# A routing chain interleaved with side work, one choice's columns built by ScalarE, activation tables loaded early and weight loads held for the first gathered rows

## The chip, the cores and the metric

The kernel runs on one core of a Trainium2 chip. The core has five engines: TensorE (PE in the profile) multiplies matrices out of SBUF into PSUM, its weight loads are listed as PEld; VectorE (DVE), ScalarE (ACT) and GpSimd (POOL) work element by element; SyncE (SP) issues transfers. Each engine runs its own instruction list in order, and they meet at semaphores. Transfers run on 16 DMA engines. TensorE's clock is granted at one of two levels, 1.2 and 2.4 GHz; the profile shows it as 0.5 and 1.0. The metric is the device time of one execution in microseconds (us).

## What is computed

A gated cross-attention block and a gated mixture of experts, both with a residual. Cut to what matters:

```
x = x + tanh(g_xattn) * xattn(layernorm(x), ctx)          # x: 16 x 112 x 256, ctx: 16 x 375 x 192, 16 heads
xf = layernorm(x) as 1792 rows of 256
probs = softmax(xf @ router_w.T)                            # 8 experts
topv, topi = top_k(probs, 2); probs = probs * mask; probs = probs / (probs.sum + 1e-9)
h = silu(xf @ gate_w[e] + gate_b[e]) * (xf @ up_w[e] + up_b[e])     # 256 -> 512
y = sum over e of probs[e] * (h @ down_w[e] + down_b[e])            # 512 -> 256
x = x + tanh(g_ffn) * y
```

## The kernel before

`attention` (to 315 us) computes the first line, batch by batch, in 20 software-pipelined steps, and leaves x, its row means and variances (mv2) and the raw router logits (routed) in SBUF. In its last steps ScalarE has only copies and squares to do.

`experts` follows. Its first part is the **routing**, written as one chain on VectorE in a layout of 112 partitions x 16 batches x 8 experts: inverse deviation (ScalarE does the Sqrt, L1245), logits, maximum, Exp on ScalarE (L1247), then twice "maximum, equal, tie-break, maximum, select" (L1420 to L1429) for the two choices of each row, and `both`, the mask of the two. From `both` TensorE counts the rows of each expert and ranks them; VectorE turns this into pos, the place of each row and choice in a list sorted by expert (L1442 to L1456). The list has 21 tiles of 256 places. To turn it round (which row stands at place p?) pos is split into chunk and offset, and TensorE multiplies two one-hot matrices: `col` (line == offset, 128 columns) and `chunks` (line == chunk, times value), for choice 1 first and then for choice 0 (L1325 to L1332). The result plus a constant is `slot_row` (L1480), the row numbers that the gather needs. Every operation of the chain is issued through `link`, which gives the operation a semaphore and waits for it at once, also where the next operation doesn't need its result.

Beside the chain ScalarE normalises x in place (XW, L1252, 16 activations), SyncE writes it to `xn_scr` in DRAM in four stores (L1180), and GpSimd, after the stores and slot_row, gathers rows with indirect transfers (L1046, two for each tile, four tiles ahead). SyncE's list ahead of the stores: weights of the first one and a half experts (w_raw x3, DL x2), small biases, zero rows, dbB; behind them DL of the third expert, and then the loop of weight loads (L1182), each waiting until VectorE has used up the buffer it goes to (e_l).

Then come the **tiles**, software-pipelined: in step c, TensorE transposes tile c (L1343), does gate and up of tile c-1 (L1366) and down of tile c-2 (L1381). ScalarE makes xH, the high part of the rows (L1263), sg = Silu(gate) (L1278), hH (L1290) and the weighted ys (L1301); VectorE makes xL (L1506), hf = (up + bias) * sg (L1527), hL (L1538) and ys (L1549). The weights, too, are split on chip while the first 8 tiles run: `high` (L1021, GH) on ScalarE and `low` (L1033, GL) on VectorE, numbered 2e for the gate and 2e+1 for the up weights of expert e, and `down_high` (L1026, DH) and `down_low` (L1040, DL). TensorE's gate and up of tile t wait for low(2t+1) (`e_l`, L1357). For expert 1, low(2) is in step 0 and low(3) in step 1 on VectorE, behind the first hf and xL.

## Time and profile before

| | |
|---|---|
| median of 3 runs (range) | 563.6 us (563.16 to 569.83) |
| profiled execution: time, span | 564.71 us, 562.9 us |
| mean granted clock of TensorE | 0.933 |
| busy: PE, PEld, DVE, ACT, POOL | 471.5, 430.2, 409.8, 317.0, 298.1 us |

The page cuts the span into 40 slices of 14.1 us; a digit is the busy share of a slice in tenths. Slices 23 to 25 (from 310 us) are the stretch of the routing:

```profile
PE   2986899999999999999988324799899999999920
DVE  4875989999999989999995585687865545555510
ACT  4651556667577566757555732777855455455410
PEclk9998999999999999999997655899999999999975
DMA  9566687775676576474311685567624433433333
```

In rows of a timeline: start in us, busy us, engine, line, operation, output<-inputs, shapes, count, and in brackets the idle time of the engine before it with what ended it.

### The profile page before, as it was taken

The page shows a single profiled execution, that of the slowest core. Times are in us where ns is not written, and L with a number is a line of the kernel's source. Part 1 is how long each engine was busy: PE and PEld are TensorE (multiplying, and loading weights), DVE is VectorE, ACT ScalarE, POOL GpSimd, SP SyncE. Part 2 cuts the span into 40 slices and gives each one's busy share as a digit, 9 for nine tenths or more (in the row PEclk, how much of TensorE's full clock was granted, in tenths as well). Part 3 has the DMA queues.
Part 4 walks back from the last instruction along what each step waited for, and adds up shares of the span by engine and source line. Part 5 has one row for each costly group of instructions (what it writes and reads, how often), then busy time and mean ns, then how long its engine had stood idle before and what let it go on. Part 6 is the DMA issues. An engine that isn't in the chain of part 4 may idle for free. (4 is left out here: it accounts for less than half of the span.)

```text
span 562.9 us, 15096 instructions
## 1 busy us (share of the span) xinstructions
PE 471.5 (84%) x4723; PEld 430.2 (76%) x4724; DVE 409.8 (73%) x872; ACT 317.0 (56%) x606; POOL 298.1 (53%) x268
## 2 busy tenths in 40 slices
PE   2986899999999999999988324799899999999920
PEld 2865898999889999999867313698799999999820
DVE  4875989999999989999995585687865545555510
ACT  4651556667577566757555732777855455455410
POOL 5093456666556666755675208034657765654440
PEclk9998999999999999999997655899999999999975
DMA  9566687775676576474311685567624433433333
GB/s 203 158 170 147 148 193 176 182 184 123 173 174 148 118 173 182 109 178 109 85 53 57 203 273 191 176 199 204 141 51 75 76 47 66 65 55 48 39 38 130
DMA packets 69022, 74.88 MB, mean 133 GB/s; under 512 B 28744, under 2 KB 57248, under 8 KB 68784
## 3 DMA queue, kind: packets, MB, share of 16 engines
q1 hardware_dynamic: 60912, 63.23, 43.1%
q0 software_dynamic: 8064, 11.06, 12.0%
q8 instruction: 27, 0.44, 0.3%
q14 instruction: 19, 0.16, 0.1%
HBM read 42.51 MB, written 14.98 MB: 102 GB/s over the span
## 5 line engine op out<-in xcount | busy, mean ns | idle before, releaser
L365 POOL TENSOR_TENSOR PL<-PT 125x448 f16<-125x448 f32 x112 | 109.5, 985 | 102.9 <-ACT PT L495 102.8
L495 ACT ACTIVATE PT<-bank 125x448 f32<-125x448 f32 x192 | 100.8, 543 | 86.2 <-PE bank L626 85.9
L783 DVE TENSOR_REDUCE mx<-bank 112x1 f32<-112x375 f32 x256 | 124.8, 538 | 18.6 <-PE bank L608 17.8
L1236 POOL DMA_INDIRECT acc_scr<-ys,slot_row x42 | 66.9, 1594 | 83.8 <-ACT ys L1301 73.7
L626 PE MATMUL bank<-QS,KS 98*125 98x256 f32 x384 | 82.8, 305 | 4.8 <-DMA QS<-nm 3.7
L608 PE MATMUL bank<-KS,QS 97*112 97x376 f32 x256 | 79.9, 352 | 2.9 <-DVE mx L783 2.2
L1527 DVE SCALAR_TENSOR_TENSOR hf<-bank,ub,sg 128x256 f32<-128x256 f32 x84 | 38.4, 482 | 51.9 <-ACT sg L1278 51.8
L1366 PE MATMUL bank<-xH,GH 128*128 128x256 f16 x336 | 66.1, 279 | 7.7 <-DVE GL L1033 3.6
L626 PEld LDWEIGHTS bank<-QS,KS 98*125 98x125 f32 x384 | 63.7, 193 | 6.5 <-DMA QS<-nm 4.0
L1366 PE MATMUL bank<-xL,GH 128*128 128x256 f16 x336 | 65.7, 278 | 0.0
L1366 PE MATMUL bank<-xH,GL 128*128 128x256 f16 x336 | 65.4, 277 | 0.0
L1046 POOL DMA_INDIRECT xt<-xn_scr,slot_row x42 | 45.4, 1082 | 30.8 <-DVE slot_row L1480 18.3
L773 DVE TENSOR_TENSOR PL<-PT 125x448 f16<-125x448 f32 x80 | 56.6, 707 | 5.6 <-ACT PT L495 5.3
L645 PE MATMUL bank<-VS,PT 125*128 125x49 bf16 x768 | 52.2, 189 | 4.0 <-POOL PL L365 1.9
L1278 ACT ACTIVATE sg<-bank,gb,inv 128x256 f32<-128x256 f32 x84 | 42.7, 560 | 20.1 <-PE bank L1366 20.0
L645 PE MATMUL bank<-VS,PL 125*128 125x49 bf16 x768 | 50.4, 186 | 0.0
L608 PEld LDWEIGHTS bank<-KS,QS 97*112 97x112 f32 x256 | 44.6, 177 | 7.2 <-DVE mx L783 5.3
L645 PEld LDWEIGHTS bank<-VS,PT 125*128 125x128 bf16 x768 | 38.2, 99 | 15.4 <-issue 3.1
L1301 ACT ACTIVATE ys<-ys,slot_weight 128x256 f32<-128x256 f32 x42 | 19.1, 500 | 42.9 <-DVE ys L1549 41.0
L1366 PEld LDWEIGHTS bank<-xH,GH 128*128 x336 | 32.3, 99 | 13.9 <-issue 9.4
L1538 DVE TENSOR_TENSOR hL<-hf,hH 128x1024 fp32r<-128x1024 f32 x21 | 25.9, 1233 | 16.9 <-ACT hH L1290 11.3
L645 PEld LDWEIGHTS bank<-VS,PL 125*128 125x128 f16 x768 | 38.1, 97 | 0.0
(214 smaller groups left out, 1033.9 us busy)
## 6 DMA issues: line engine op xcount, KB each, us to landing
KS<-kH SPq DMA_DIRECT2D x128, 94.0 KB, 2.7
KS<-kL SPq DMA_DIRECT2D x64, 94.0 KB, 2.2
QS<-q_scr SPq DMA_DIRECT2D x96, 56.0 KB
ctx_sb<-in_ctx SPq DMA_DIRECT2D x16, 281.2 KB
wsq<-in_L_ffn_gate_w SPq DMA_DIRECT2D x8, 512.0 KB, 3.9
wsq<-in_L_ffn_up_w SPq DMA_DIRECT2D x8, 512.0 KB, 5.0
w_raw<-in_L_ffn_gate_w SPq DMA_DIRECT2D x8, 512.0 KB, 4.2
w_raw<-in_L_ffn_up_w SPq DMA_DIRECT2D x8, 512.0 KB, 3.9
```

The source lines that it names most:

```text
L365: pool.tensor_tensor(PL[:, 2 * k:2 * k + 2, :, 0:N], PT[:, 2 * k:2 * k + 2, :, 0:N], PH[:, 2 * k:2 * k + 2, :, 0:N], ALU.subtract).then_in ...
L495: act.activation(PT[:, 2 * k:2 * k + 2, :, 0:N].rearrange("p a e i -> p (a e) i"), psST[k % 2][0:JP].rearrange("p (a i) -> p a i", i=NI)[: ...
L608: pe.matmul(psS[hd % SBANKS][0:N, 0:MP], QS[u][0:RM, hd // 2, hd % 2, 0:N], KS[u][0:RM, hd // 2, :], start=True, stop=True).then_inc(p_S, 1)
L626: mm = pe.matmul(psST[k % 2][0:JP, 2 * NI * a:2 * NI * (a + 1)], KS[u][0:RM + 1, p, JP * t:JP * (t + 1)], QS[u][0:RM + 1, p, :, :].rearran ...
L645: mm = pe.matmul(psO[0][:, VW * (hd % 8):VW * (hd % 8 + 1)], P[:, JT * p + t, e, :], VT[:, u, t, hd, :], start=(part == 0 and t == 0), sto ...
L773: dve.tensor_tensor(PL[:, 2 * k:2 * k + 2, :, 0:N].rearrange("p a e i -> p (a e) i"), PT[:, 2 * k:2 * k + 2, :, 0:N].rearrange("p a e i -> ...
L783: dve.tensor_reduce(mx[:, hd:hd + 1], psS[hd % SBANKS][0:N, 0:M], AX.X, ALU.max).then_inc(v_max, 1)
L1046: pool.indirect_dma_start(xt[:, t % XR, k, :], None, xn_scr, bass.IndirectOffsetOnAxis(ap=slot[:, TH * t + k:TH * t + k + 1].bitcast(U32), ...
L1236: pool.indirect_dma_start(acc_scr, bass.IndirectOffsetOnAxis(ap=slot[:, TH * t + k:TH * t + k + 1].bitcast(U32), axis=0), ys[:, u, k, :], ...
L1278: act.activation(sg[:, f, :], bG[f // FB][:, TS * (f % FB):TS * (f % FB + 1)], ACT.Silu, bias=gb[:, bass.ds(e * FC + f, 1)], scale=inv[:, ...
L1366: mm = pe.matmul(bank[:, TS * (f % FB):TS * (f % FB + 1)], w.rearrange("p o f -> p (o f)"), x[:, u, k, :], start=(n == 0 and k == 0), stop ...
L1527: dve.scalar_tensor_tensor(out=hf[:, f, :], in0=bU[f // FB][:, TS * (f % FB):TS * (f % FB + 1)], scalar=ub[:, bass.ds(e1 * FC + f, 1)], in ...
```

## The change

- **Chain.** `link` is split in `mark` (gives the semaphore) and the wait. The sum of the exponentials, m12, den and rden move from behind `both` in between the links of the two choices. Behind pos the small operations are issued in an order in which neighbours don't depend on each other, and each waits only for what it reads.
- **Columns.** `col` of choice 0 is made by ScalarE: 16 activations |offset - line| of 112x128 and one Relu(1 - that) over all 2048 elements. `offset` becomes F32. TensorE waits for ScalarE there.
- **Tables.** Two activations with an unread result: a Sqrt of two elements in step 17 of attention, and a Silu behind the first down_high.
- **Weights.** SyncE waits for the first tile's gathered rows (l_x[0]) before its loop of weight loads; low(3) moves on VectorE from step 1 to step 0.

```
+                    if isinstance(i, int) and NB * i + c == B + 1:
+                        act.activation(v["unread"][:], ident[:, 0:2], ACT.Sqrt)
...
-            chunk, offset = tmp("k_chunk", [N, 2, B], BF16), tmp("k_offset", [N, 2, B], BF16)
+            chunk, offset = tmp("k_chunk", [N, 2, B], BF16), tmp("k_offset", [N, 2, B], F32)
...
                 load_down(sp, 2)
+                sp.wait_ge(l_x[0], 16 * TH)
                 for n in range(WB, 2 * E):
...
+                act.wait_ge(e_off, 1)
+                act.wait_ge(q_k, 9)
+                for b in range(B):
+                    ins = act.activation(col[:, 0, b, :], line[:], ACT.Abs, bias=offset[:, 0, b:b + 1], scale=-1.0)
+                ins.then_inc(a_col, 1)
+                act.wait_ge(a_col, 1)
+                act.activation(col[:, 0].rearrange("i b l -> i (b l)"), col[:, 0].rearrange("i b l -> i (b l)"),
+                               ACT.Relu, bias=ones[0:N, 0:1], scale=-1.0).then_inc(a_col, 1)
                 act.wait_ge(e_sc, 1)
                 high(act, 0)
                 high(act, 1)
                 down_high(act, 0)
+                act.activation(v["unread"][:], ident[:, 0:2], ACT.Silu)
...
-                    pe.wait_ge(e_col, n + 1)
+                    if k == 1:
+                        pe.wait_ge(e_col, 1)
+                    else:
+                        pe.wait_ge(a_col, 2)
...
-                link(dve.tensor_reduce(r["sum"][:], R["exp"][:], AX.X, ALU.add))
-                link(dve.tensor_tensor(r["m12"][:], r["m1"][:], r["m2"][:], ALU.add))
-                link(dve.scalar_tensor_tensor(out=r["den"][:], in0=r["sum"][:], scalar=1e-9, in1=r["m12"][:],
-                                              op0=ALU.mult, op1=ALU.add))
-                link(dve.reciprocal(r["rden"][:], r["den"][:]))
+                dve.wait_ge(e_r, n_rden)
...
+                n_mid = mark(dve.tensor_scalar(k2["mid"][:], k2["pos"][:], -63.5, 1.0 / 128, ALU.add, ALU.mult))
+                n_near = mark(dve.tensor_scalar(k2["near"][:], k2["pos"][:], 0.5 - TS / 2, 1.0 / TS, ALU.add, ALU.mult))
+                dve.wait_ge(e_r, n_mid)
+                n_chunk = mark(dve.tensor_scalar(chunk[:], k2["mid"][:], EDGE, EDGE, ALU.add, ALU.subtract))
...
-                                if arrived(i, c):
+                                if arrived(i, c) and UN * i + c > 1:
                                     low(dve, 2 * (UN * i + c) + 1)
...
                     if arriving(i, c):
                         low(dve, 2 * (UN * i + c + 1))
+                        if not has(i, c, 1):
+                            low(dve, 2 * (UN * i + c + 1) + 1)
```

ScalarE's list from the first activation of the expert phase to the first tile, before; XW is the normalised x, GH and DH are high parts of weights, xH the rows of tile 0, k_offset is offset:

```order
L1245 ACT_TABLE_LOAD
L1245 ACTIVATE rstd<-veps 112x16 [waits dve_ve2]
L1247 ACT_TABLE_LOAD
L1247 ACTIVATE r_exp<-r_low 112x128 [waits dve_low]
L1252 ACTIVATE XW<-XW,shift,rstd 112x256 [waits attention_stored0,dve_shift]
L1252 ACTIVATE XW<-XW,shift,rstd 112x256 x12
L1252 ACTIVATE XW<-XW,shift,rstd 112x256 [waits attention_stored1]
L1252 ACTIVATE XW<-XW,shift,rstd 112x256 x2
L1021 ACTIVATE GH<-w_raw,sc 128x1024 [waits gate_in0,dve_scale]
L1021 ACTIVATE GH<-w_raw,sc 128x1024 [waits gate_in1]
L1026 ACTIVATE DH<-DL 128x1024 [waits down_in0]
L1263 ACTIVATE xH<-bank 128x512 [waits pe_tileT]
```

The same place in the changed kernel:

```order
L1251 ACTIVATE rstd<-veps 112x16 [waits dve_ve2]
L1253 ACT_TABLE_LOAD
L1253 ACTIVATE r_exp<-r_low 112x128 [waits dve_low]
...
L1258 ACTIVATE XW<-XW,shift,rstd 112x256 x2
L1263 ACTIVATE col<-line,k_offset 112x128 [waits pool_constants,dve_offset]
L1263 ACTIVATE col<-line,k_offset 112x128 x15
L1266 ACTIVATE col<-col,ones 112x2048 [waits act_col]
L1025 ACTIVATE GH<-w_raw,sc 128x1024 [waits gate_in0,dve_scale]
L1025 ACTIVATE GH<-w_raw,sc 128x1024 [waits gate_in1]
L1030 ACTIVATE DH<-DL 128x1024 [waits down_in0]
L1272 ACT_TABLE_LOAD
L1272 ACTIVATE unread<-ident 128x2
```

One table load is gone at the head, 17 activations stand between XW and the first weights, and a table load stands ahead of xH.

VectorE's list over steps 0 and 1 of the tiles, before; the step border is the TENSOR_LOAD of the tile's expert, hf is the product with sg:

```order
L1511 TENSOR_TENSOR both_w<-xt,slot_choice 128x4 [waits tile_in0]
L1514 TENSOR_REDUCE slot_weight<-both_w 128x2 [waits dve_two_weights]
L1040 TENSOR_TENSOR DL<-DL,DH 128x1024 [waits act_down_high]
L1033 SCALAR_TENSOR_TENSOR GL<-w_raw,sc,GH 128x1024 [waits act_high]
L1151 TENSOR_LOAD tile_e
...
L1506 SCALAR_TENSOR_TENSOR xL<-bank,xH 128x512 [waits act_tile_x]
L1511 TENSOR_TENSOR both_w<-xt,slot_choice 128x4 [waits tile_in1]
L1514 TENSOR_REDUCE slot_weight<-both_w 128x2 [waits dve_two_weights]
L1033 SCALAR_TENSOR_TENSOR GL<-w_raw,sc,GH 128x1024 [waits act_high]
L1527 ISA [waits act_silu]
L1527 SCALAR_TENSOR_TENSOR hf<-bank,ub,sg 128x256
```

The same place in the changed kernel:

```order
L1553 TENSOR_TENSOR both_w<-xt,slot_choice 128x4 [waits tile_in0]
L1556 TENSOR_REDUCE slot_weight<-both_w 128x2 [waits dve_two_weights]
L1044 TENSOR_TENSOR DL<-DL,DH 128x1024 [waits act_down_high]
L1037 SCALAR_TENSOR_TENSOR GL<-w_raw,sc,GH 128x1024 [waits act_high] x2
L1156 TENSOR_LOAD tile_e
...
L1548 SCALAR_TENSOR_TENSOR xL<-bank,xH 128x512 [waits act_tile_x]
L1553 TENSOR_TENSOR both_w<-xt,slot_choice 128x4 [waits tile_in1]
L1556 TENSOR_REDUCE slot_weight<-both_w 128x2 [waits dve_two_weights]
L1569 ISA [waits act_silu]
L1569 SCALAR_TENSOR_TENSOR hf<-bank,ub,sg 128x256
```

The GL behind tile 1's xL now stands in step 0, behind the other one.

SyncE's list behind the stores, before and then changed, where the first load of the loop gets one more wait (tile_in0 is l_x[0]):

```order
L1180 DMA xn_scr<-XW 112x4x258 [waits act_xn2] x3
L1015 DMA DL<-in_L_ffn_down_w 128x4x256
L1012 DMA w_raw<-in_L_ffn_up_w 128x2x512 [waits dve_wlow]
L1015 DMA DL<-in_L_ffn_down_w 128x4x256
L1012 DMA w_raw<-in_L_ffn_gate_w 128x2x512 [waits dve_wlow]
```

```order
L1185 DMA xn_scr<-XW 112x4x258 [waits act_xn2] x3
L1019 DMA DL<-in_L_ffn_down_w 128x4x256
L1016 DMA w_raw<-in_L_ffn_up_w 128x2x512 [waits dve_wlow,tile_in0]
L1019 DMA DL<-in_L_ffn_down_w 128x4x256
L1016 DMA w_raw<-in_L_ffn_gate_w 128x2x512 [waits dve_wlow]
```

Nothing changed its place there; every later load stands behind the new wait.

## Rows read from the trace of the kernel before

**Rows 1.** Windows: busy us (instructions) of each engine, then PEclk, DMA share, GB/s.

```profile
333.00:335.00 2.00, 0.09 (x2) 0.00 (x0) 2.00 (x2) 0.00 (x0) 0.00 (x0) 0.50 1.04 323
```

**Rows 2.** Timeline of ScalarE, end of attention and routing.

```profile
307.96 0.42 ACT L449 ACTIVATE xc<-XW 112x256 f32<-112x256 f32 x1 [1.02 <-DVE XW L845]
...
315.08 1.28 ACT L1245 ACT_TABLE_LOAD   x1 [0.98 <-PEq L246]
...
317.92 0.31 ACT L1247 ACTIVATE r_exp<-r_low 112x128 f32<-112x128 f32 x1
318.13 7.95 ACT L1252 ACTIVATE XW<-XW,shift,rstd 112x256 f32<-112x256 f32 x16
325.99 2.17 ACT L1021 ACTIVATE GH<-w_raw,sc 128x1024 f16<-128x1024 f32 x2
```

**Rows 3.** Timeline of VectorE, routing chain.

```profile
322.17 0.28 DVE L1432 TENSOR_REDUCE s_sum<-r_exp 112x16 f32<-112x128 f32 x1
...
323.19 0.40 DVE L1438 SCALAR_TENSOR_TENSOR XW<-s_m,tg,s_rden 112x16 f32<-112x16 f32 x2
...
326.17 0.18 DVE L1458 TENSOR_SCALAR k_mid<-k_pos 112x32 f32<-112x32 f32 x1
...
327.71 0.86 DVE L1469 TENSOR_TENSOR chunks<-line,k_chunk 112x672 f16<-112x672 bf16 x1
...
333.25 2.29 DVE L1475 TENSOR_TENSOR col<-line,k_offset 112x2048 bf16<-112x2048 bf16 x1
...
336.44 0.20 DVE L1480 TENSOR_TENSOR slot_row<-bank,spare 128x42 int32<-128x42 f32 x1 [0.90 <-PE bank L1329]
```

**Rows 4.** Source line L1180 in 325.9 to 327, the last store.

```profile
L1180 SPq DMA_DIRECT2D xn_scr<-XW x1: 305/305/305, 326.1 to 326.1; - x1
...
DMA to landing us min/median/max: 8.8/8.8/8.8
```

**Rows 5.** Timeline round the gather; last, DMA busy tenths from 337, slices of 0.2 us.

```profile
337.57 1.17 POOL L1046 DMA_INDIRECT xt<-xn_scr,slot_row  x1 [18.28 <-DVE slot_row L1480]
...
338.15 2.47 DVE L1033 SCALAR_TENSOR_TENSOR GL<-w_raw,sc,GH 128x1024 f16<-128x1024 f32 x2
339.04 1.22 POOL L1046 DMA_INDIRECT xt<-xn_scr,slot_row  x1 [0.30 <-issue]
339.45 0.39 SPq L1012 DMA_DIRECT2D w_raw<-in_L_ffn_up_w  x1
...
340.54 1.22 DVE L1040 TENSOR_TENSOR DL<-DL,DH 128x1024 fp32r<-128x1024 f32 x1
340.57 2.01 POOL L1046 DMA_INDIRECT xt<-xn_scr,slot_row  x1 [0.30 <-issue]
...
343.90 1.11 PE L1343 MATMUL bank<-ident,xt 128*128 128x128 f32 x4 [7.51 <-DMA xt<-xn_scr,slot_row]
...
DMA  0000000000009351072149899998999999987899
```

**Rows 6.** The chain (first row, start and us), ScalarE and TensorE at tiles 0, 1.

```profile
346.52 6.32 PE bank L1366 x24
...
352.96 1.28 ACT L1278 ACT_TABLE_LOAD   x1 [4.29 <-PE bank L1366]
...
358.17 0.61 PE L1366 MATMUL bank<-xH,GH 128*128 128x256 f16 x2 [3.56 <-DVE GL L1033]
```

**Rows 7.** Timeline of VectorE, hf of tiles 0, 1, 2 and 3.

```profile
354.97 0.94 DVE L1527 SCALAR_TENSOR_TENSOR hf<-bank,ub,sg 128x256 f32<-128x256 f32 x2 [4.89 <-ACT sg L1278]
...
363.46 0.88 DVE L1527 SCALAR_TENSOR_TENSOR hf<-bank,ub,sg 128x256 f32<-128x256 f32 x2 [1.16 <-ACT sg L1278]
...
373.54 0.88 DVE L1527 SCALAR_TENSOR_TENSOR hf<-bank,ub,sg 128x256 f32<-128x256 f32 x2 [1.61 <-ACT sg L1278]
...
383.07 0.88 DVE L1527 SCALAR_TENSOR_TENSOR hf<-bank,ub,sg 128x256 f32<-128x256 f32 x2 [1.60 <-ACT sg L1278]
```

**Rows 8.** DMA issues of the page: KB each, median us to landing.

```profile
w_raw<-in_L_ffn_up_w SPq DMA_DIRECT2D x8, 512.0 KB, 3.9
```

More of the change, by code:

```diff
@@ L1456, in _ @@
                 link(dve.tensor_reduce(k2["pos"][:], pick[:], AX.X, ALU.add))
-                link(dve.tensor_scalar(k2["mid"][:], k2["pos"][:], -63.5, 1.0 / 128, ALU.add, ALU.mult))
-                link(dve.tensor_scalar(chunk[:], k2["mid"][:], EDGE, EDGE, ALU.add, ALU.subtract))
-                link(dve.scalar_tensor_tensor(out=offset[:], in0=chunk[:], scalar=-128.0, in1=k2["pos"][:],
-                                              op0=ALU.mult, op1=ALU.add))
-                link(dve.tensor_scalar(k2["near"][:], k2["pos"][:], 0.5 - TS / 2, 1.0 / TS, ALU.add, ALU.mult))
@@ L1463, in _ @@
-                link(dve.tensor_scalar(k2["tile"][:], k2["near"][:], EDGE, EDGE, ALU.add, ALU.subtract))
-                link(dve.tensor_tensor(k2["back"][:], row[:].unsqueeze(1).to_broadcast([N, 2, B]), k2["pos"][:],
-                                       ALU.subtract))
-                link(dve.scalar_tensor_tensor(out=value[:], in0=k2["tile"][:], scalar=float(TS), in1=k2["back"][:],
-                                              op0=ALU.mult, op1=ALU.add))
-                for k in (1, 0):
-                    link(dve.tensor_tensor(chunks[:, k, :, k, :],
-                                           line[:, 0:NH].unsqueeze(1).to_broadcast([N, B, NH]),
-                                           chunk[:, k, :].unsqueeze(2).to_broadcast([N, B, NH]), ALU.is_equal))
+                n_mid = mark(dve.tensor_scalar(k2["mid"][:], k2["pos"][:], -63.5, 1.0 / 128, ALU.add, ALU.mult))
@@ new lines, in _ @@
+                n_near = mark(dve.tensor_scalar(k2["near"][:], k2["pos"][:], 0.5 - TS / 2, 1.0 / TS, ALU.add, ALU.mult))
+                dve.wait_ge(e_r, n_mid)
+                n_chunk = mark(dve.tensor_scalar(chunk[:], k2["mid"][:], EDGE, EDGE, ALU.add, ALU.subtract))
+                dve.wait_ge(e_r, n_near)
+                n_tile = mark(dve.tensor_scalar(k2["tile"][:], k2["near"][:], EDGE, EDGE, ALU.add, ALU.subtract))
+                dve.wait_ge(e_r, n_chunk)
+                dve.scalar_tensor_tensor(out=offset[:], in0=chunk[:], scalar=-128.0, in1=k2["pos"][:],
+                                         op0=ALU.mult, op1=ALU.add).then_inc(e_off, 1)
@@ new lines, in _ @@
+                n_back = mark(dve.tensor_tensor(k2["back"][:], row[:].unsqueeze(1).to_broadcast([N, 2, B]),
+                                                k2["pos"][:], ALU.subtract))
+                n_place = {}
+                for k in (1, 0):
+                    n_place[k] = mark(dve.tensor_tensor(chunks[:, k, :, k, :],
+                                                        line[:, 0:NH].unsqueeze(1).to_broadcast([N, B, NH]),
+                                                        chunk[:, k, :].unsqueeze(2).to_broadcast([N, B, NH]),
+                                                        ALU.is_equal))
+                    if k == 1:
+                        dve.wait_ge(e_r, n_back)
+                        link(dve.scalar_tensor_tensor(out=value[:], in0=k2["tile"][:], scalar=float(TS),
+                                                      in1=k2["back"][:], op0=ALU.mult, op1=ALU.add))
+                    dve.wait_ge(e_r, n_place[k])
```

39 lines of the change are left out of this document (30 added, 9 removed).

## The prediction

> **What bounds the kernel now.** I read the page first (busy shares, then the chain that ended last), then the timeline of each engine between the end of attention (315 us) and the sixth tile of the experts (395 us), then the windows with the DMA share, then what each engine waited for. The chain of the expert phase is TensorE's matmuls from the first gate matmul on. Ahead of it lies the routing, where TensorE does almost nothing: at 343.90 it has waited 7.51 us for the first gathered rows [rows 5]. So the stretch 315 to 344 is latency, and it has two strands. One is VectorE's routing chain, which ends with slot_row at 336.44 [rows 3]. The other is SyncE's queue: the DMA engines are full at 333 to 335 and empty from 337 to 339.4 [rows 1, 5], and the last of the four stores of normalised rows, issued at 326.1, lands 8.8 us later, at 334.9 [rows 4]. The gather waits for both. In this trace slot_row comes 1.7 us after the stores, so VectorE decides, but only by that much. Behind the gather there are two more places: ScalarE loads the Silu table at 352.96, in front of the first gate activation, and TensorE waits 3.56 us for GL before it starts the second tile at 358.17, where a pair of gate matmuls then takes 0.61 us [rows 6]. From the third tile on, as long as weights are being split, hf of one tile and the next are 9.5 us apart (373.54, 383.07), with VectorE busy but for 1.6 us of waiting on ScalarE [rows 7].
>
> **Table loads.** The Sqrt load (1.28 us at 315.08) moves into attention's last steps, where ScalarE idles 1.02 us (307.96) and has no Exp left [rows 2]. Sqrt then starts at about 315.3 and not 316.37, so everything behind it comes 1.05 us sooner. The Exp load behind it still fits beside VectorE's four operations up to Exp at 317.92. The Silu load leaves the path between the first gate matmuls and sg: 1.28 us [rows 2, 6], 1.3 us with its gap. It is covered by ScalarE's idle time before the rows arrive. The Trainium skill (ScalarE: Activation LUTs, "What ACT_TABLE_LOAD costs") gives about 2.66 us for a switch with its drain. The trace disagrees: from the load's start at 352.96 to hf at 354.97 there is room for 1.28 us of load and 0.7 us of sg alone, and by the page's price the forecast would be 1.4 us lower, an estimate.
>
> **VectorE's chain.** sum, m12, den and rden leave the path between both and the weights: 322.17 to 323.19, 1.0 us [rows 3]. They come back between links. A link waits some 0.1 us at its end for its own result, so a 16-element operation rides there for nothing, and the 128-element sum costs 0.1 to 0.3 us. Net 0.6 to 0.9; I take 0.6, since the count also waits for TensorE. The seven small links from mid (326.17) to chunks (327.71) take 1.54 us; after, three of them are on the path: 0.65, less 0.1 for value: gain 0.8. The second col (2.29 us at 333.25) goes to ScalarE. VectorE would be through with the second chunks at 333.25 - 1.05 - 0.6 - 0.8 = 330.8.
>
> **ScalarE's columns.** They stand behind the 16 activations of XW, which end at 326.08 - 1.05 = 325.0; offset is there at 325.1. Sixteen activations of 112x128 cost between 0.31 us (the lone Exp of that size) and 0.50 us (XW, twice the elements, two pointers) each: 5.0 to 7.95 us. I take 5.0, since the element count is that of the first. Relu over 2048 elements is at most the two GH of 1024 together, 2.17 us; I take 2.1 [rows 2]. So col is ready at 332.2 (at worst 335.3), later than VectorE's 330.8. This is the new tail of the chain. From the end of col to slot_row there were 0.9 us (335.54 to 336.44), so slot_row comes at 333.1, 3.3 us sooner, or at worst 336.2. The three weight activations queued behind it start at about 332.2 and not 325.99 and need 3.2 us; VectorE's GL needs the first at 334.8, and that is met.
>
> **What ends the wait now.** The four stores sit in a queue that was full before they were issued. Issuing them 1 to 2 us sooner puts no byte ahead of another, so they land at 334.9 as before, 1.8 us after slot_row. Of 3.3 us gained on the chain, 1.7 to 2.0 count. POOL takes 0.3 us (its gap between two fetches) to 0.9 us (336.64 to 337.57) to begin; with 0.6 the first fetch starts at 335.5, the second at 337.0.
>
> **The held weights.** Before, SyncE issues three weight loads from 339.45, and the second fetch, begun at 339.04, is complete only at 343.9, 4.86 us later. The first fetch had an empty queue: its traffic is over by 340.2, 2.6 us after its start [rows 5]. With 0.4 us for the landing I take 3.0 for a fetch alone. That gives 340.0 for the second one. Against this: the fetch at 340.57, beside VectorE's DL subtraction (340.54), took 2.01 us, where later ones take about 1. After the change that DL subtraction falls at 337 to 338.5, on the second fetch. I charge 0.85: rows complete at 340.9, 3.0 us sooner than 343.9. The bounds are 340.0 and 342.8.
>
> **The first tiles.** From rows to the first gate matmul, 2.6 us as before; then 6.32 us for 24 of them at the low clock; then sg without the load. hf of tile 0 comes 3.0 + 1.3 = 4.3 us sooner than 354.97. In this step VectorE's GL for the second up weights is gone, but it only frees time in which VectorE waits for ScalarE, so the step's last GL ends 4.3 us sooner too, at 362.30 - 4.3 = 358.0. What the move does change is TensorE: GL is done in the step before, at about 348, and the second tile waits only for xL (about 352.2), so its 3.56 us stall shrinks under 1 us, and the low clock behind it should go too. Not all of that is gain: hf of tile 1 waited 1.16 us for sg, and now starts when VectorE is free, at 358.0. Gain 4.3 + 1.16 = 5.5. The step from there to hf of tile 2 took 10.08 us, 0.55 over the steady 9.53, waiting on TensorE and ScalarE; that comes back too: 6.0 us. From tile 2 on, 9.53 us a step is VectorE's and ScalarE's own and stays, and so does TensorE's pace behind it.
>
> The loads that are held: issued at 340.9 to 341.7 they land in about 3.9 us each [rows 8], three behind one another by 347.6; ScalarE's fourth GH can wait till 348 without touching sg (349.9), and the next needs its weights at 351.3. Cover 3 us or more; beyond it each us costs one.
>
> Sum: 6.0 us. The profiled execution has a span of 562.9 and a time of 564.7; after, 556.9 and 558.7. Its time is 1.1 us above the median of the runs, 563.6, so for the median I forecast **557.6 us**.
>
> **The rivals.**
> - *The queue does not hold the stores.* Issued sooner, they land sooner, and slot_row decides: fetch at 333.1 + 0.2 + 0.9 = 334.2 and not 335.5; 556.3 us. The full DMA share speaks against it. Chance 0.08.
> - *VectorE locks POOL out.* If every two-input operation of VectorE stops the descriptors, the first fetch runs at 338.5, the second ends at 340.8, rows at 342.8: gain 1.9 us smaller, 559.5 us. For it: the 2.01 us fetch. Against it: GL's pair (338.15, 2.47 us) and two fetches ran beside each other, at 1.17 and 1.22 us. The Trainium skill (SBUF — State Buffer, "SBUF: two separate sides") has this as an exclusive lock against an operation with two SBUF inputs; by that rule this rival holds, and the trace agrees only for DL. Chance 0.10.
> - *The hold brings nothing.* The second fetch's 4.86 us are its own: rows at 337.0 + 0.85 + 4.86 = 342.7, 559.4 us. Chance 0.10.
> - *The held weights come late.* If the first lands after 9.6 us and not 3.9 (a queued store took 8.8), ScalarE's fourth GH stands before sg until 351.7 and 1.8 us go: 559.4 us. Chance 0.06.
> - *Slower.* The same place, far end: sg of tile 0 comes 1.2 us after that landing, so the whole gain is lost when the load takes 15 us (340.9 + 15 = 355.9); with 17 us, 565.6 us. Some 2.3 MB wait then, under 7 us at the rate of this stretch, which speaks against it. Chance 0.02.
>
> **How the numbers follow.** The forecast has 0.62, with its own range 555.6 to 559.4: 1.5 us for when the clock rises in the first 24 matmuls, 0.9 for the collision at the second fetch. The rest, 0.02, is what I do not see. From 553.9 (the first rival with a luckier clock) to 560.9 (two of the later ones in part together) holds 8 in 10. 2%, about what a measurement of this kernel can tell from no change, is 11.3 us, and no case reaches it: faster 0.03, same 0.96, slower 0.01.
>
> **What would show it.** No table load between 315.0 and 315.3 nor ahead of the first sg; stores landing at about 335 with slot_row before them, near 333; the second fetch complete 3 to 4 us after its start; TensorE's wait before the second tile under 1 us, at the full clock; hf 9.5 us apart from tile 1 on. I am wrong if the stores land before slot_row, if ScalarE's columns take over 7 us, or if hf of tile 1 does not wait for VectorE.

## The result and the profile after

| | before | changed |
|---|---|---|
| median of 4 runs each, side by side (range) | 564.55 us (563.16 to 569.83) | 560.43 us (558.61 to 561.69) |
| ratio, 95% interval | | 0.9883 [0.9846, 0.992] |
| profiled execution: time, span | 564.71, 562.9 us | 561.69, 559.9 us |
| mean granted clock of TensorE | 0.933 | 0.927 |

The changed kernel is 0.8 to 1.5% faster, which is under the 2% that the prediction took as its border for "same". Two more comparisons on other occasions, five rounds each, gave 0.9889 [0.9848, 0.9929] and 0.992 [0.9892, 0.9949]: 6.3 and 4.5 us. The forecast, 557.6 us with a range of 553.9 to 560.9, holds the 560.43 near its upper end.

The slices of the page after (14.0 us each; a digit is tenths busy, PEclk tenths of the full clock):

```profile
PE   2986999999999999999988524899899999999920
DVE  5965889998999989999996486687865545555410
ACT  4642556676676567667555595677855455455510
PEclk9988999999999999999997555899999999999975
DMA  8566677775567466555403296576734433433333
```

ScalarE is busy for 9 and 5 tenths of the slices 24 and 25, where it had 3 and 2, and TensorE has 8 tenths in slice 26, where it had 7. The low clock of slices 23 to 25 is still there. Since the stretch ahead of the routing shifts from one profile to the next, places are given from here on as a **distance from the start of VectorE's first operation of the expert phase** (veps: at 315.12 in the profile before, 318.74 after, by the same view). The places, read from the timelines:

| us from veps | before | before, again | forecast | after | again | again2 |
|---|---|---|---|---|---|---|
| veps itself, in the span | 315.12 | 319.38 | 315.1 | 318.74 | 319.41 | 318.40 |
| both | 6.84 | 6.85 | 5.8 | 5.99 | 6.00 | 5.99 |
| mid | 11.05 | 11.07 | 9.4 | 9.53 | 9.53 | 9.52 |
| chunks of choice 0 done | 18.21 | 18.22 | 15.7 | 15.88 | 15.88 | 15.88 |
| col of choice 0 done | 20.41 | 20.43 | 17.1 | 17.00 | 17.00 | 17.00 |
| slot_row | 21.32 | 21.33 | 18.0 | 17.90 | 17.90 | 17.90 |
| last store landed | 19.82 | 20.21 | 19.8 | 19.31 | 20.10 | 20.07 |
| first fetch | 22.45 | 22.46 | 20.4 | 19.59 | 20.38 | 20.35 |
| rows complete | 28.78 | 28.73 | 25.8 | 24.70 | 25.96 | 26.00 |
| hf of tile 0 | 39.85 | 38.51 | 35.6 | 35.37 | 34.65 | 33.94 |
| hf of tile 1 | 48.34 | 47.01 | 42.8 | 42.56 | 42.44 | 41.73 |
| hf of tile 2 | 58.42 | 57.22 | 52.4 | 52.45 | 51.96 | 51.25 |
| end of the span | 247.76 | 245.96 | 241.8 | 241.21 | 240.77 | 240.30 |

(The forecast's column is its own times less 315.12, for "both" 6.84 - 1.05, for mid 0.6 less again; "rows complete" is TensorE's first transpose.)

The timeline of ScalarE after, to be held against [rows 2]:

```profile
308.41 1.28 ACT L429 ACT_TABLE_LOAD   x1
...
318.95 0.21 ACT L1251 ACTIVATE rstd<-veps 112x16 f32<-112x16 f32 x1 [1.23 <-DVE veps L1420]
...
320.70 7.95 ACT L1258 ACTIVATE XW<-XW,shift,rstd 112x256 f32<-112x256 f32 x16
328.93 4.78 ACT L1263 ACTIVATE col<-line,k_offset 112x128 bf16<-112x128 bf16 x16 [0.28 <-DVE k_offset L1497]
333.74 2.00 ACT L1266 ACTIVATE col<-col,ones 112x2048 bf16<-112x2048 bf16 x1
335.65 2.17 ACT L1025 ACTIVATE GH<-w_raw,sc 128x1024 f16<-128x1024 f32 x2
...
338.79 1.28 ACT L1272 ACT_TABLE_LOAD   x1
```

Nothing stands ahead of the root any more; the sixteen Abs took 4.78 us (forecast 5.0) and the Relu 2.00 (2.1). VectorE [rows 3]:

```profile
328.28 0.18 DVE L1490 TENSOR_SCALAR k_mid<-k_pos 112x32 f32<-112x32 f32 x1
...
336.65 0.20 DVE L1522 TENSOR_TENSOR slot_row<-bank,spare 128x42 int32<-128x42 f32 x1 [2.02 <-PE bank L1347]
```

VectorE now waits 2.02 us for the product behind ScalarE's columns. The window that answers [rows 1], and the last store [rows 4]:

```profile
333.00:335.00 2.00, 1.28 (x16) 1.12 (x16) 1.59 (x2) 1.97 (x4) 0.00 (x0) 0.50 1.12 280
```

```profile
L1185 SPq DMA_DIRECT2D xn_scr<-XW x1: 305/305/305, 328.7 to 328.7; - x1
...
DMA to landing us min/median/max: 9.4/9.4/9.4
```

The DMA engines are full again, and the store takes 9.4 us where it took 8.8: issued 10.0 after veps and not 11.0, it lands at 19.3 (19.8 before). GpSimd and TensorE round the gather [rows 5]:

```profile
338.34 1.17 POOL L1050 DMA_INDIRECT xt<-xn_scr,slot_row  x1 [15.28 <-DMA xn_scr<-XW]
339.81 1.86 POOL L1050 DMA_INDIRECT xt<-xn_scr,slot_row  x1 [0.30 <-issue]
...
343.45 1.11 PE L1361 MATMUL bank<-ident,xt 128*128 128x128 f32 x4 [6.84 <-DMA xt<-xn_scr,slot_row]
```

The releaser in the brackets has changed from slot_row to the stores: they are late now. The rows are complete 3.6 us after the start of the second fetch (4.9 before). VectorE's hf of the tiles 0 to 3 [rows 7]:

```profile
354.12 0.94 DVE L1569 SCALAR_TENSOR_TENSOR hf<-bank,ub,sg 128x256 f32<-128x256 f32 x2 [3.29 <-ACT sg L1293]
...
361.30 0.87 DVE L1569 SCALAR_TENSOR_TENSOR hf<-bank,ub,sg 128x256 f32<-128x256 f32 x2
...
371.19 0.88 DVE L1569 SCALAR_TENSOR_TENSOR hf<-bank,ub,sg 128x256 f32<-128x256 f32 x2 [1.60 <-ACT sg L1293]
...
380.72 0.88 DVE L1569 SCALAR_TENSOR_TENSOR hf<-bank,ub,sg 128x256 f32<-128x256 f32 x2 [1.61 <-ACT sg L1293]
```

hf of tile 1 waits for nothing but VectorE, and from there the steps are 9.5 us again after one of 9.9. One sign of the prediction is not there: TensorE's wait before the second tile was to be under 1 us, and the clock behind it full. Here are that wait and the matmuls round it:

```profile
353.36 0.38 PE L1384 MATMUL bank<-xH,GL 128*128 128x256 f16 x2
355.79 0.60 PE L1384 MATMUL bank<-xH,GH 128*128 128x256 f16 x2 [2.05 <-DVE xL L1548]
356.19 0.63 PE L1384 MATMUL bank<-xL,GH 128*128 128x256 f16 x2
```

A pair takes 0.38 us ahead of the wait and 0.60 to 0.63 behind it, where the mean granted clock is 0.51 (355.8 to 359.1). In the two further profiles of the same kernel, below, TensorE does not wait there at all. In the span the expert phase is 6.6 us shorter and began 3.6 us later; the profiled execution is 3.0 us better, and not 6. That is the first thing to explain.

### The profile page after: what moved, and what is told of

It is laid out like the page before. It is cut to its first block and busy times, and to the rows that moved or that the text cites. A ratio compares the mean times of both kernels' runs of the same rounds, so it can differ in the third digit from the quotient of the medians.

```text
span 559.9 us, 15117 instructions
## 1 busy us (share of the span) xinstructions
PE 475.1 (85%) x4723; PEld 433.4 (77%) x4724; DVE 407.3 (73%) x871; ACT 324.5 (58%) x625; POOL 297.7 (53%) x268
## 5 line engine op out<-in xcount | busy, mean ns | idle before, releaser
L1293 ACT ACTIVATE sg<-bank,gb,inv 128x256 f32<-128x256 f32 x84 | 42.8, 561 | 23.8 <-PE bank L1384 18.1
L1580 DVE TENSOR_TENSOR hL<-hf,hH 128x1024 fp32r<-128x1024 f32 x21 | 25.9, 1233 | 16.9 <-ACT hH L1305 12.4
```

What stands on the lines that cost most here:

```text
L1293: act.activation(sg[:, f, :], bG[f // FB][:, TS * (f % FB):TS * (f % FB + 1)], ACT.Silu, bias=gb[:, bass.ds(e * FC + f, 1)], scale=inv[:, ...
```

## The experiments

Each kernel ran five rounds beside the kernel before; the ratio is to that. On the first occasion the kernel before had a median of 565.32, on the second 564.57, on the third 564.53 us. before_again, again and again2 change nothing; the others are the changed kernel with the edits shown, cut to what matters.

### Are the 3.6 us ahead of the phase the change's?

The same two kernels, profiled again.

**again** (changed kernel):

> The changed kernel once more, as the yardstick on this chip. Two readings of its first profile: attention ended 3.6 us later there (the expert phase began at 318.70 and not 315.07) because the low clock happened to last through its end; or the change itself, by the Sqrt table load put into it, makes attention longer. The first expects the expert phase to begin anywhere from 314 to 319 us, with the granted clock in 306 to 314 us deciding. Counted from that beginning, the first xt rows should be complete at 24.7 us, sg of tile 0 at 34.7.

**before_again** (kernel before):

> The kernel before, profiled once more, with nothing changed. In its first profile the expert phase began at 315.1 us; in all nine profiles of kernels with the change, or most of it, it began at 317.5 to 319.7. If that was the luck of one execution (theory), it begins at 316 to 319.5 here and its span is 564 to 567; if the change's idle tensor moves addresses and so costs 3 us ahead of the phase (rival), it begins at about 315 again. The expert phase itself should last 247 to 248.5 us again, and the first group of matmuls, 7.7 us in the first profile, about 6 us if that length was of one execution.

**again2** (changed kernel, on before_again's occasion):

> The changed kernel once more, beside order2 on the same chip: 560 us, as in again, with the expert phase beginning at 317.5 to 319.7 us and lasting 240.5 to 241.5. Rows complete at 24.7 to 26.0 us after its start.

Measured: again 560.09 us, ratio 0.9889 [0.9848, 0.9929]; before_again 564.95 us, 1.0006 [0.9978, 1.0033]; again2 560.73 us, 0.992 [0.9892, 0.9949]. The expert phase of before_again began at 319.38 us, later than in two of the three profiles of the changed kernel. So the 3.6 us were the luck of the one execution that was profiled before. The windows of 0 to 100 and of 300 to 316 us show a part of why: the mean granted clock was 0.97 and 0.71 in the first profile before, and in each of the others lower in one of the two (before_again 0.97 and 0.63, after 0.95 and 0.53, again 0.91 and 0.77, again2 0.97 and 0.50). From veps on before_again took 245.96 us and not 247.76. Against the mean of both (246.9) the changed kernel's three (mean 240.8) are 6.1 us shorter; the forecast was 6.0, and the three timed comparisons gave 6.6, 6.3 and 4.5. In two of the five profiles, before and after, ScalarE lost time ahead of tile 0 to a wait described under "The first tiles" below; without these two the phase is 5.2 us shorter in again and 5.7 in again2 than in before_again.

### What is late at the gather: the columns, the chain or the stores?

**col_vector** makes both column matrices on VectorE, as before:

```
-                for b in range(B):
-                    ins = act.activation(col[:, 0, b, :], line[:], ACT.Abs, bias=offset[:, 0, b:b + 1], scale=-1.0)
...
-                        pe.wait_ge(a_col, 2)
+                    pe.wait_ge(e_col, n + 1)
...
+                    dve.tensor_tensor(col[:, k], line[:].unsqueeze(1).to_broadcast([N, B, 128]),
```

> The changed kernel with choice 0's columns made by VectorE again, as before the change. Theory Q, the queue of stores decides when the gather starts: slot_row comes about 1.1 us later (19.1 us from the start of the expert phase, against 17.95), still ahead of the last store's landing (19.4), so the time stays within 0.3 us of the changed kernel. Theory V, the chain of VectorE and ScalarE decides: 1.1 us slower.

**col_and_waits** also waits after every operation of the chain:

```
             def mark(ins):
...
+                    dve.wait_ge(e_r, n_chain[0])
```

> As the run with VectorE's columns, and besides every operation of the chain waits for itself again (the order of the changed kernel is kept). Both theories expect slot_row about 2.4 us later than in the changed kernel, at 20.4 us or more from the start of the expert phase. Theory Q: 1 us of it lies behind the stores, so first fetch at about 21.3 and not 19.64, 1.3 to 1.9 us slower. Theory V: 2.4 us slower, and slower than the former run by as much as slot_row is later.

**no_sqrt** leaves out the early Sqrt of two elements, so the table is loaded ahead of the root:

> The changed kernel without the Sqrt table load inside attention. Chain: Exp and all behind it come 1.05 us later from the start of the expert phase, XW ends at 11.0 and slot_row comes at 18.95. By the queue theory the rows come 0 to 0.3 us later, for slot_row is still ahead of the stores (19.3 to 20.4). Rival A, that load made attention longer: the expert phase then begins earlier here, and the kernel is faster. Rival B, the chain decides: 1 us slower. I expect within 0.5 us of the changed kernel.

Measured: col_vector 558.71 us, 0.9883 [0.9836, 0.993]; col_and_waits 561.48, 0.9932 [0.9904, 0.996]; no_sqrt 559.79, 0.9904 [0.9868, 0.994]. The kernel again, on the occasion of the first two, had 0.9889. In col_vector slot_row came 1.08 us later (18.98) and GpSimd still waited for the stores:

```profile
339.60 2.14 POOL L1050 DMA_INDIRECT xt<-xn_scr,slot_row  x1 [17.76 <-DMA xn_scr<-XW]
```

The stores landed at 21.79 there, later than in any other profile, with nothing changed ahead of them; over all the kernels with the old order they land at 19.3 to 21.8. In no_sqrt slot_row came 0.92 later (18.82), the stores at 19.62, and the rows not later but 1.4 us sooner than in again (24.51), with a first fetch that lost nothing to VectorE. Its phase began at 319.02, no earlier than that of after or again2, so nothing shows that the early load makes attention longer. In col_and_waits slot_row came 4.1 us later and not 2.4 as expected, at 22.01 after veps; that is 0.7 us later than before, since the operations put in between the links now each wait as well (both at 7.64, and at 5.99 in the changed kernel). It was at last what GpSimd waited for:

```profile
342.27 1.17 POOL L1050 DMA_INDIRECT xt<-xn_scr,slot_row  x1 [18.77 <-DVE slot_row L1511]
```

It lost 1.5 us in the phase against again (242.28 and 240.77); timed, the intervals of the two overlap, but on that occasion five of again's six runs are faster than every one of col_and_waits' twelve. So about two of the 3.4 us by which the chain is shorter lie behind the stores. Either of two edits, the columns or the Sqrt load, can be undone and the time doesn't tell. What was seen to count is the columns undone together with the links; the Sqrt load was not undone together with anything.

**stores_first** takes the two transfers in front of the stores away from there (the second expert's down weights and dbB, 128 partitions of all down biases), behind the stores, some of them behind the hold:

```
-                load_down(sp, 1)
...
-                sp.dma_start(dbB[:], down_b.unsqueeze(0).to_broadcast([128, E, DIM])).then_inc(i_db, 16)
...
-                load_down(sp, 2)
+                load_down(sp, 1)
+                sp.wait_ge(l_x[0], 16 * TH)
...
+                    if n == WB:
+                        load_down(sp, 2)
...
+                    if n == WB + 2:
+                        sp.dma_start(dbB[:], down_b.unsqueeze(0).to_broadcast([128, E, DIM])).then_inc(i_db, 16)
```

> The changed kernel with SyncE's list in another order: the load of expert 1's down weights stands behind the four row stores, and dbB (1 MB) and expert 2's down weights behind the first gathered rows. 1.5 MB less lie ahead of the stores and 0.5 MB less behind them. Theory Q (the full queue holds the stores' landing): they land 3 to 4 us sooner, at 16 to 17 from the start of the expert phase, slot_row (17.9) decides, the first fetch starts at 18.2 to 19.0 and not 19.6 to 20.4; 1 to 2 us faster than the changed kernel. Theory V: stores were never the last, no change. If the moved loads come late for down and ys of tile 0, it is slower; they are needed 10 us after the rows at the earliest.

Measured: 559.45 us, 0.9898 [0.9869, 0.9928]. The last store landed 16.42 us after veps, 3.7 us sooner than in again and 2.9 sooner than in any profile with the old order, slot_row decided (GpSimd's wait of 14.71 us ends at it), and the rows were complete at 23.60, 2.4 us sooner. That the queue ahead of the stores set their landing is shown; order2 and order2_split, below, land them at 16.9 as well. But of the gain at the rows most was given back two steps on, on ScalarE and VectorE:

```profile
352.65 1.15 ACT L1025 ACTIVATE GH<-w_raw,sc 128x1024 f16<-128x1024 f32 x1 [2.60 <-DMA w_raw<-in_L_ffn_gate_w]
```

```profile
354.39 0.94 DVE L1571 SCALAR_TENSOR_TENSOR hf<-bank,ub,sg 128x256 f32<-128x256 f32 x2 [3.36 <-ACT sg L1295]
```

The held weights now come late, as in the prediction's fourth rival: hf of tile 0 was 3.5 us ahead of again, of tile 1 1.1, the end 0.3. The 1 to 2 us that were expected are not in the time.

**order2** keeps the edits of stores_first, but issues the next gate-and-up weights ahead of the down weights that were moved:

```
-                    if n % 2 and n // 2 + 2 < E:
-                        load_down(sp, n // 2 + 2)
+                    if n in (WB + 1, WB + 2):
+                        load_down(sp, n - 2)
...
+                    if n > WB + 2 and n % 2 and n // 2 + 1 < E:
+                        load_down(sp, n // 2 + 1)
```

> The changed kernel with the stores of the rows in front of the down weights in the sync engine's queue, and with the gate-and-up weights that follow issued ahead of the second down weight. Theory: the stores land 16.4 us after the start of the expert phase as in stores_first, the first rows are complete at 23.6 (again: 26.0), and since the weights that stores_first waited 2.60 us for now come earlier, little is given back: hf1 at 40.3 to 41, and some 1.5 to 2 us faster than the changed kernel. Rival: the weights come late again (the queue is full either way), hf1 at 41.3 or more, and within 1 us of stores_first.

**order2_split** is order2 and gives four of ScalarE's sixteen column batches to VectorE, since slot_row is what is late in order2:

```
-                for b in range(B):
+                for b in range(BA):
...
+                dve.tensor_tensor(col[:, 0, BA:B], line[:].unsqueeze(1).to_broadcast([N, B - BA, 128]),
+                                  offset[:, 0, BA:B].unsqueeze(2).to_broadcast([N, B - BA, 128]), ALU.is_equal
+                                  ).then_inc(e_col, 1)
```

> order2, and the last four of the sixteen column batches made by VectorE in one operation after the chain, ScalarE the first twelve. In order2 the addresses of the rows (slot_row, at 17.9) come after the stores' landing (16.4), so that the columns decide: the addresses should come 0.5 to 0.7 us sooner (17.2 to 17.4), with the fetches and rows behind them, and the time be 0.5 us below that of order2 or within its interval. Rival: VectorE's part on the path costs what ScalarE's saves, and slot_row stays at 17.7 to 18.

Measured: order2 560.25 us, 0.9921 [0.9893, 0.9949], the same as again2 beside it (0.992) and not 1.5 to 2 us faster; order2_split 557.72 us, 0.9889 [0.986, 0.9919]. In order2 the stores landed at 16.94, the rows were complete at 23.64, and hf of tile 1 came at 39.69, 2.0 us ahead of again2, somewhat better than expected. Then the next weights came late,

```profile
359.88 1.15 ACT L1025 ACTIVATE GH<-w_raw,sc 128x1024 f16<-128x1024 f32 x1 [1.66 <-DMA w_raw<-in_L_ffn_gate_w]
```

and 0.8 us were left at the end, of which the timing shows nothing. The wait for weights moves on by a step with each gain at the front. In order2_split slot_row came at 17.38, 0.52 us sooner, as expected, and the rows at 23.12; there the rows of the second tile were late,

```profile
348.75 0.66 PE L1366 MATMUL bank<-ident,xt 128*128 128x128 f32 x4 [1.74 <-DMA xt<-xn_scr,slot_row]
```

and at tile 2 and at tile 7 it stood 0.2 us behind order2. Its median is the lowest of all kernels run, 3 us under again2 on the same occasion, but the intervals overlap. Its phase is 1.8 us shorter than that of again2 (238.51 against 240.30), and 1.0 of that is a lead over order2 which it does not yet have at tile 7 (97.09 against 96.86), so it comes from places that no edit touches. Whether the split is worth anything stays open.

### What is the hold worth?

**no_hold** removes SyncE's wait:

```
                 load_down(sp, 2)
-                sp.wait_ge(l_x[0], 16 * TH)
```

> The changed kernel without SyncE's wait for the first rows. Theory H, the weight loads delay the second fetch: three loads are issued at about 21 us from the start of the expert phase, the second fetch takes 4.9 us and not 3.6, and the kernel is 1.2 us slower. Rival, the fetch's time is its own (VectorE's DL subtraction in front of its descriptors): no difference, or 0.3 us faster since weights come sooner.

Measured: 563.12 us, 0.9955 [0.9928, 0.9982], against 0.9889 [0.9848, 0.9929] of again on the same occasion. The two intervals overlap by 0.0001; but five of again's six runs are faster than every one of no_hold's twelve, so the hold does gain. The chain of again (start, us, what) and then of no_hold:

```profile
329.34 10.16 DMA xn_scr<-XW
...
341.65 3.67 DMA xt<-xn_scr,slot_row
...
347.99 5.18 PE bank L1384 x24
```

```profile
327.70 10.34 DMA xn_scr<-XW
...
340.00 5.86 DMA xt<-xn_scr,slot_row
...
348.53 4.10 PE bank L1383 x24
```

The stretch from the second fetch to complete rows grows from 3.67 to 5.86 us, by 2.2. (The prediction's step: 3.85 with the hold, 4.86 + 0.85 = 5.7 without.) In this pair half of it comes back at once: the first 24 matmuls take 4.10 us and not 5.18, since the clock rose 33.5 us after veps in both, 4.9 us behind the first of them in again and 2.7 in no_hold. That is no rule, though. From complete rows to the transposes behind these 24 matmuls no_hold takes 6.6 us, and the three profiles of the changed kernel take 6.6 (after), 7.6 (again) and 6.9 (again2): where the clock rises differs from execution to execution by as much. Against the three, no_hold is 1.0 to 1.8 us late at tile 1 and 0.1 to 1.0 at the end. The timed loss, 3.7 us, is larger than the traces explain. Each trace is of one execution, too: that of no_hold was the fastest of its twelve, that of again the slowest of its six. So the place, the 2.2 us there and that there is a gain are shown; what the hold is worth at the end lies between 0.1 us by the traces and 3.7 by the timing.

### The Silu load and low(3)

**no_silu** leaves out the early Silu; **low_back** puts low(3) back into step 1:

```
-                act.activation(v["unread"][:], ident[:, 0:2], ACT.Silu)
```

> The changed kernel without the early Silu load. A table load of 1.28 us stands before the first sg again; everything behind it hangs on sg of tile 0, since hf of tile 1 waits for VectorE, which waits for hf of tile 0. Expected 1.3 us slower (0.23%). By the page's price of 2.66 us for a switch it would be 2.7 us slower. Rival: hidden by the wait for TensorE's first 24 matmuls, 0.

```
-                                if arrived(i, c) and UN * i + c > 1:
+                                if arrived(i, c):
...
-                        if not has(i, c, 1):
-                            low(dve, 2 * (UN * i + c + 1) + 1)
```

> The changed kernel with low(3), the GL of expert 1's up weights, back in step 1, behind tile 1's xL. The prediction charged the move with 1.7 us of the 6.0: TensorE waits for it before tile 1 and hf of tile 1 starts late. Expected from it: hf of tile 1 8.5 to 8.9 us behind hf of tile 0 and not 7.8 (seen once more in the changed kernel), TensorE idle over 3 us before tile 1, at the low clock after it, and the kernel 1.0 to 2.0 us slower than the changed one. Rival: VectorE and ScalarE set the pace from tile 1 on anyway, under 0.3 us.

Measured: no_silu 561.08 us, 0.9938 [0.9915, 0.996]; low_back 561.45 us, 0.9924 [0.9895, 0.9952]. Neither can be told from the three ratios of the changed kernel, and none of them was taken beside these two. The traces say more, once the clock is taken out: it rose 0.9 us sooner in no_silu than in again (32.6 and 33.5 us after veps), which hides a part of the load there. So this table counts from the first transpose behind the first 24 matmuls of tile 0:

| us from that transpose | before_again | again | again2 | no_silu | low_back |
|---|---|---|---|---|---|
| the transpose, in the span | 355.58 | 353.00 | 351.29 | 351.41 | 353.29 |
| hf of tile 0 | 2.31 | 1.06 | 1.05 | 2.31 | 1.08 |
| hf of tile 1 | 10.80 | 8.85 | 8.84 | 9.50 | 8.86 |
| hf of tile 2 | 21.02 | 18.37 | 18.36 | 19.02 | 18.39 |

Without the early Silu load hf of tile 0 is 1.25 us late, and of tiles 1 and 2 still 0.65. With low(3) back nothing is late, although TensorE began tile 1 1.25 us later than in again (37.90 and not 36.65): the over 3 us of idle TensorE and the 1 to 2 us that were expected of low_back did not come. In before_again, with neither edit, 1.95 us are lost at tile 1 and 2.65 at tile 2. What made the step long before is a row of waits, here on TensorE, ScalarE and VectorE of before_again:

```profile
361.08 0.40 PE L1366 MATMUL bank<-xH,GH 128*128 128x256 f16 x2 [2.29 <-DVE GL L1033]
```

```profile
365.61 1.02 ACT L1278 ACTIVATE sg<-bank,gb,inv 128x256 f32<-128x256 f32 x2 [1.81 <-PE bank L1366]
```

```profile
366.38 0.88 DVE L1527 SCALAR_TENSOR_TENSOR hf<-bank,ub,sg 128x256 f32<-128x256 f32 x2 [1.17 <-ACT sg L1278]
```

and the windows of before_again and of low_back just behind TensorE's wait (the sixth figure behind the comma is PEclk):

```profile
362.20:365.60 3.40, 3.40 (x18) 2.55 (x16) 3.01 (x3) 1.60 (x2) 0.00 (x0) 0.51 0.49 142
```

```profile
357.60:360.50 2.90, 2.90 (x27) 2.62 (x28) 2.55 (x4) 2.90 (x4) 0.00 (x0) 1.00 0.71 170
```

Before, TensorE idled 2.29 us in front of tile 1 (3.56 in [rows 6]) and then worked at half the clock, 18 matmuls in 3.4 us. In low_back low(3) ends as long after hf of tile 0 as before (3.0 us), yet TensorE idles only 1.03 us,

```profile
357.56 0.41 PE L1384 MATMUL bank<-xH,GH 128*128 128x256 f16 x2 [1.03 <-issue]
```

because without the Silu load hf of tile 0, and low(3) behind it, follow TensorE's last matmul of tile 0 1.3 us sooner. The clock stays up (27 matmuls in 2.9 us) and hf has nothing to wait for. So either of the two edits, the Silu load or low(3), takes away the wait of hf of tile 1. Of the 1.95 us there, the Silu load has 0.65 for itself, low(3) nothing, and 1.3 come with whichever of them is made. That both undone together would bring the wait back is argued from before_again and was not run.

## Why the prediction was right, point by point

- **Table loads.** Sqrt: forecast 1.05; between no_sqrt and again slot_row moved by 0.92, and the load stood there with 1.28 us. Nearly right. The 1.28 us for a load was right too: in no_silu it took 1.28 at 351.70, with sg directly behind it, and hf of tile 0 was 1.25 us late. The other half of that step failed. I let the 1.3 us of the Silu load run through to hf of tile 0 and on; but a tile has two pairs of hf, and the second waits for TensorE in any case (1.23 us in again, 0.62 in no_silu), so that 0.65 us are left at tile 1.
- **VectorE's chain.** Forecast 0.6 for sum to rden, and from mid to the chunks 0.8. In no_sqrt, where both kernels load the Sqrt table alike, mid came at 10.45 and before at 11.05: 0.60, with the interleaved operations paid. From mid to the chunks of choice 0 7.16 before, 6.35 after: 0.81. Both right.
- **ScalarE's columns.** Ready at 17.1, came at 17.00; slot_row at 18.0, came at 17.90. Right, and the choice of 5.0 among 5.0 to 7.95 by the element count was right (4.78).
- **The stores decide.** Right: landing at 19.3 to 20.1 (forecast 19.8) with slot_row 1.4 to 2.2 us before it, and shown by col_vector, no_sqrt and stores_first. The pick-up was 0.28 us and not 0.6, the landing of again and again2 0.3 later; the first fetch began at 20.4, as forecast. The rival that the queue does not hold the stores is out.
- **VectorE locks POOL out.** Here the reasoning failed, though the 0.85 us charged for the collision was near: the first two fetches together lost 0.9 us in after and 1.3 in again and again2. I had counted a fetch that ran beside GL's pair as evidence against a lock, and charged DL alone. The fetches of low_back and VectorE's operations beside them show what happens:

```profile
339.62 1.98 POOL L1050 DMA_INDIRECT xt<-xn_scr,slot_row  x1 [15.63 <-DMA xn_scr<-XW]
341.90 1.82 POOL L1050 DMA_INDIRECT xt<-xn_scr,slot_row  x1 [0.30 <-issue]
```

```profile
339.28 2.47 DVE L1037 SCALAR_TENSOR_TENSOR GL<-w_raw,sc,GH 128x1024 f16<-128x1024 f32 x2
341.67 1.22 DVE L1044 TENSOR_TENSOR DL<-DL,DH 128x1024 fp32r<-128x1024 f32 x1
```

  The first fetch begins inside the first GL. That one is through at 340.47, where the second GL begins, and 340.47 + 1.13 is the end of the fetch (341.60). The second fetch begins inside DL; DL is through at about 342.80, and 342.80 + 0.92 is the end of that fetch (343.72). A fetch alone takes 0.94 to 0.97 us, the first of them 1.17. So a fetch that begins while VectorE is in an operation with two inputs in SBUF stands until that operation ends. One that has begun ahead of it is not held up: the first fetch of [rows 5], at 337.57, began before GL; the second, at 339.04, began 0.3 us before the first GL ended (the pair's halfway, 339.35), hence 1.22. An operation counts as through here 0.1 us ahead of its recorded end, where VectorE's next one starts. Of the first three fetches in each of the fourteen profiles 26 begin within a GL or DL; each ends 0.95 us (a first fetch 1.17) after that operation is through, to within 0.04 us, and none of the sixteen others takes more than 0.97 or, as a first fetch, 1.17. The collision in the profile after was with the second GL (339.55 to 340.75; 340.75 + 0.94 = 341.69, recorded 341.67), not with DL. The Trainium skill (SBUF — State Buffer, "SBUF: two separate sides") says that whoever starts first holds the lock for its whole instruction; these rows agree for the fetch that comes second. In the other direction they don't: GL's operations last 1.27 us also where a fetch was running when they began. So the rival's mechanism holds, at a chance of 0.10, but its price (1.9 us more) was too high: the first fetch lost only 0 to 1.0 us to it, depending on where in GL the stores land.
- **The hold.** 3.85 us from the second fetch to the rows, measured 3.6 to 3.8; without it 5.9 (5.7). The rival that it brings nothing is out. In all eleven profiles with the hold the rows are complete 1.8 to 1.9 us behind the end of the second fetch's instruction, in the three without it 3.6 to 4.1. The first held load landed 3.9 us after its issue in again, as forecast, the third after 8.0, 34.9 us after veps where 32.5 was forecast; the fourth GH waited 0.17 us for the first of them, and sg of tile 0 for none, so the rival that they come late did not come true. (The sum of the last rival is off by its own rule: a load of 15 us puts sg of tile 0 at 340.9 + 15 + 1.2 = 357.1, 7.2 us late and not 6.0.)
- **The first tiles.** The sum came out (hf of tile 1 at 42.8, measured 41.7 to 42.6), the working did not. 6.32 us for the first group was one execution's: it is 5.03 in the chain of before_again and 4.10 to 5.30 in those of again, again2, no_hold, low_back, no_silu, no_sqrt and col_vector. In the profile after there is another 5.33 us that the chain cannot name, ahead of the first sg, when the matmuls it needs had long been issued:

```profile
347.90 5.33 another core or an unknown queue
```

  The transposes behind those 24 matmuls began at 350.02, sg at 353.39. Twice in fourteen profiles ScalarE waited like that behind those matmuls, 3.0 us too long in after and 1.3 in before. What it waits for is not settled. That hf of tile 0 came at 35.37 there, 0.2 us from the forecast, is luck: rows 1.1 us sooner and a first group 2.4 us shorter (3.95 and not 6.32) than forecast nearly cancel this wait. The wait is also why the sign at the second tile failed there: hf, and xL behind it, came late for TensorE. The step that failed is the credit in "gain 4.3 + 1.16": the 1.16 us and the 0.55 behind it were given to low(3), which by itself is worth nothing at tile 1 or 2, and come as well with the Silu load. The size of the two edits together was near, 3.0 us forecast behind the rows and 2.65 between before_again and again at tile 2. The clock fell a second time, at tile 1, in before, before_again and after, and in none of the other eleven.
- **The size.** 557.6 was made from a profile that began the phase 4.3 us sooner than before_again. That did not enter the difference, but the three comparisons put the median at 560.1 to 560.7, against kernels before of 564.5 to 565.3: 3.8 to 5.2 us by the medians, 4.5 to 6.6 by the ratios. The forecast's 6.0 is within the second and above the first, and some of its 2.8 us of error is the median of three runs from which it started, 563.6, where larger samples gave 564.5 to 565.3.

## What to carry to other kernels

Ask of a latency chain which of its strands is late, and by how much: here the routing was made 3.4 us shorter and two of them did nothing, because a store behind a full transfer queue landed when it landed. The cheapest edits were in the order of transfers. One wait that keeps bulk loads away from a latency-bound gather gave 2.2 us at the gather, and two loads moved behind the stores would give 1.1 to 2.4 more (23.60 against 24.70 in after and 25.96 in again), but what is moved back becomes late itself within two steps. Before two edits are credited with their gains one by one, see whether either alone takes away the same wait; and take a stretch that you compare from two profiles of the same kernel, since this one's start moved by over 4 us between executions.

## What the runs showed of the hardware

- A gather's rows land late when ordinary loads run beside it: from the end of the second fetch's instruction to complete rows 1.9 us with the queue held (343.47 to 345.37 in again), 4.1 us with three weight loads issued meanwhile (341.82 to 345.91 in no_hold). The eleven profiles with the hold have 1.8 to 1.9 us, the three without it 3.6 to 4.1.
- TensorE's clock rose 28.9 to 36.0 us after veps, and 2.7 to 5.4 us after the first gate matmul, at a fixed distance from neither. The same kernel in three executions (after, again, again2) had 2.8, 4.9 and 3.4 us from that matmul, so one pair of profiles does not tell what sooner rows gain or lose by the clock.
- A gather's fetch on GpSimd that begins during a VectorE operation with two SBUF inputs of 128x1024 stands until it ends: 1.22 to 2.14 us and not 0.95 to 1.17. In again the first two fetches lost 0.4 and 0.9 us to this, on the path. By these rows a GL or DL that starts just before a fetch costs that fetch up to 1.1 us (2.01 and not 0.95); no kernel here moved them away from the fetches.
